# Second attention of a one-core adaLN, attention and mixture kernel: the loop over bodies of 256 tokens written anew

## What is computed

```python
def _tc_rmsnorm(x, t, gw, gb, bw, bb):
    g = (t @ gw.T + gb)[:, None, :]
    b = (t @ bw.T + bb)[:, None, :]
    inv_rms = jax.lax.rsqrt(jnp.mean(x * x, axis=-1, keepdims=True) + EPS)
    return g * x * inv_rms + b
# attention of 16 heads of 16 features, over the 64 tokens of a sequence
attn = jnp.einsum('blhd,bmhd->bhlm', q, k) / scale
p = jax.nn.softmax(attn, axis=-1)
o = jnp.einsum('bhlm,bmhd->blhd', p, v).reshape(B, L, D)
return o @ Wo.T
```

## Time and profile before

| what | us |
|---|---|
| median of 3 runs | 1128.04 |
| the three runs | 1119.44, 1128.04, 1129.88 |
| the profiled execution | 1130.07 |
| its span | 1128.4 |
| first attention, stretch of the span | 360 to 523 |
| second attention, stretch of the span | 523 to 694 |

### The profile page before, as it was taken

The page is one execution under the profiler, slowest core; times in us unless marked ns, Lnnn a source line. Parts: engine busy times, 40 slices in busy tenths (PEclk is TensorE's granted clock), DMA queues, the critical chain, the costliest instruction groups (busy, mean ns, idle before and its releaser), DMA issues. The chain is left out here.

```text
span 1128.4 us, 20924 instructions
## 1 busy us (share of the span) xinstructions
PE 929.7 (82%) x7712; PEld 792.6 (70%) x7712; DVE 651.0 (58%) x1034; ACT 525.1 (47%) x1017; POOL 194.8 (17%) x203
## 2 busy tenths in 40 slices
PE   5269999999992787884899894999988975877897
PEld 4259999999991565663677773999987862332476
DVE  2747777677760555562787875544434765221497
ACT  3046676767750233453767675333324432322332
POOL 1032232322203334421232311000000000000011
PEclk8579999999996778897999998999998976887899
DMA  8178898989951243230000000000009512999121
GB/s 317 38 250 299 317 339 301 343 324 312 336 173 42 52 141 71 49 60 21 1 1 0 0 1 1 1 1 0 1 5 354 240 65 78 410 426 381 33 72 47
DMA packets 73529, 166.57 MB, mean 148 GB/s; under 512 B 42872, under 2 KB 48248, under 8 KB 63208
## 3 DMA queue, kind: packets, MB, share of 16 engines
q1 hardware_dynamic: 62832, 122.80, 30.9%
q0 software_dynamic: 9008, 40.58, 9.8%
q10 hardware_dynamic: 1608, 2.12, 0.5%
HBM read 151.05 MB, written 12.32 MB: 145 GB/s over the span
## 5 line engine op out<-in xcount | busy, mean ns | idle before, releaser
L581 DVE TENSOR_TENSOR moew_wl<-moew_raw,moew_wh 128x1024 fp32r<-128x1024 f32 x92 | 110.1, 1220 | 21.4 <-issue 19.9
L84 PE MATMUL moe_pH<-moe_hh,moew_wh 128*128 128x256 f32 x368 | 103.2, 281 | 1.2 <-DVE moe_hl L590 1.2
L86 PE MATMUL moe_pH<-moe_hl,moew_wh 128*128 128x256 f32 x368 | 102.6, 279 | 0.0
L85 PE MATMUL moe_pH<-moe_hh,moew_wl 128*128 128x256 f32 x368 | 102.6, 279 | 0.0
L543 ACT ACTIVATE moe_ht<-moe_pH,moe_b 128x256 f32<-128x256 f32 x184 | 76.6, 467 | 39.4 <-PE moe_pH L86 39.4
L590 DVE TENSOR_TENSOR moe_hl<-moe_ht,moe_hh 128x512 fp32r<-128x512 f32 x92 | 63.8, 694 | 52.2 <-ACT moe_hh L552 51.9
L2456 POOL TENSOR_TENSOR tok_xb<-k_x,k_rows 128x512 f32<-128x512 f32 x8 | 10.2, 1272 | 425.6 <-POOLq L71 363.7
L84 PEld LDWEIGHTS moe_pH<-moe_hh,moew_wh 128*128 128x128 f32 x368 | 69.1, 188 | 1.4 <-DVE moe_hl L590 1.4
L86 PEld LDWEIGHTS moe_pH<-moe_hl,moew_wh 128*128 128x128 f32 x368 | 69.2, 188 | 0.0
L85 PEld LDWEIGHTS moe_pH<-moe_hh,moew_wl 128*128 128x128 f32 x368 | 69.0, 187 | 0.0
L528 ACT ACTIVATE moew_wh<-moew_raw 128x1024 fp32r<-128x1024 f32 x44 | 46.3, 1055 | 45.8 <-DMA moew_raw<-in_w 45.1
(11 more groups left out here) (364 smaller groups left out, 2875.3 us busy)
## 6 DMA issues: line engine op xcount, KB each, us to landing
moew_raw<-in_w SPq DMA_DIRECT2D x46, 512.0 KB
moew_wh<-in_w POOLq DMA_DIRECT2D x23, 1024.0 KB, 8.3
moew_raw<-in_w SPq DMA_DIRECT2D x23, 1024.0 KB
ring<-in_w_slot SPq DMA_DIRECT2D x11, 2048.0 KB, 19.2
...
```

The source lines that it names most:

```text
L84: nc.tensor.matmul(out, ah, bh, start=start, stop=False)
L85: nc.tensor.matmul(out, al, bh, start=False, stop=False)
L86: return nc.tensor.matmul(out, ah, bl, start=False, stop=stop)
L581: v.tensor_tensor(wl[a][l][:, n], raw_w[a][l][:, n], f32(wh[a][l][:, n]), ALU.subtract).then_inc(wl_ok[l], 1)
```

## The change

`attention_second` replaces the second attention. It takes over the three helpers of the first attention and its form of softmax.

- Scores: head masks are now 4 copies of the keys (three on VectorE, one on ScalarE), and a product covers 64 features, 64 queries and 4 heads; four such products sit in the four quarters of the array.
- Values, weights times values, and output are direct fp32 products; queries and keys stay split. The tokens are split once, not twice over, and used for queries and keys.
- Values carry a column of ones, so the same product gives the sum of the weights. VectorE takes its reciprocal and multiplies the result, which has tokens on partitions; TensorE turns the result back, ScalarE copies it, and the product with the output weights follows one body behind. GpSimd no longer divides.
- Largest, difference and exponential take all 16 heads of a tile in one step of 1024 elements.
- The output weights are loaded anew by 8 DMAs in an order that fits the new layout. The split and the copy of the old ones go.
- All 8 bodies are written out.

```diff
@@ -1060,545 +1060,375 @@
+def attention_second(nc, g, dr):
...
+        kx = sb("kx", [P, KD, HR, PB])
+        m4 = sb("m4", [P, HR])
...
+        @block.sync
+        def _(sp):
+            for r in range(4):
+                for k in range(KD):
+                    sp.dma_start(wo[32 * r:32 * r + 32, k, :], dr.wo4[64 * (r % 2):64 * (r % 2) + 32, 2 * k + r // 2, :]).then_inc(wo_in, 16)
+            sp.wait_ge(wo_in, 16 * 4 * KD)
...
+            def biased(i):
+                pool.wait_ge(u1_ok, i + 1)
+                if i > 0:
+                    pool.wait_ge(v_ps, i)
+                    pool.wait_ge(ul_ok, i)
+                nc.gpsimd.tensor_tensor(batches(u2[:, :, :]), batches(u1[:, :, :]), bc(g.ada[:, 1, :, 4 * i:4 * i + 4], 3, S), ALU.add).then_inc(u2_ok, 1)
...
-            def softmax_end(t):
-                for c in range(2):
-                    pool.wait_ge(rc_ok, 2 * t + c + 1)
-                    after(pool, pt_ps, 2 * t + c - 1)
-                    nc.gpsimd.tensor_tensor(pn[c][:, :, :], ex[c][:, :, :], bc(rc[c][:, :], 2, S), ALU.mult).then_inc(pn_ok, 1)
...
-                pe.wait_ge(k_sb, NK * (i + 1))
-                pe.wait_ge(oh_ok, 2 * t + 2)
-                pe.wait_ge(ol_ok, 2 * t + 2)
-                for j in range(4):
-                    last = mm3(nc, b2[:, 0:D], oh[:, j, :, :].rearrange("p b s -> p (b s)"), ol[:, j, :, :].rearrange("p b s -> p (b s)"),
...
+            def keys(i):
+                pe.wait_ge(uh_ok, i + 1)
+                pe.wait_ge(ul_ok, i + 1)
+                features(pC, 1).then_inc(k_ps, 1)
+
+            def queries(i):
+                if i > 0:
+                    pe.wait_ge(v_dve, i)
+                    pe.wait_ge(v_act, i)
+                features(pD, 0).then_inc(q_ps, 1)
+
+            def values(i):
+                pe.wait_ge(u2_ok, i + 1)
+                pe.wait_ge(q_sb, i + 1)
+                values_of(nc, pV, u2, g.w_small[:, W_V2]).then_inc(v_ps, 1)
+
+            def scores(t):
+                i = t // 2
+                pe.wait_ge(q_sb, i + 1)
+                pe.wait_ge(kx_dve, NM * (i + 1))
+                pe.wait_ge(kx_act, (HR - NM) * (i + 1))
+                if t >= 2:
+                    pe.wait_ge(df_ok, t - 1)
+                scores_of(nc, pS[t % 2], qT, kx, t % 2 * P, t % 2 * P).then_inc(s_ps, 1)
+
+            def turn_weights(t):
+                i = t // 2
+                pe.wait_ge(ex_ok, t + 1)
+                for n, bank in enumerate((pA, pB)):
+                    if n == 0 and t > 0:
+                        pe.wait_ge(ot_ok, t)
+                    if n == 1 and t % 2 == 0 and i >= 2:
+                        pe.wait_ge(o_sb, i - 1)
+                    if n == 1 and t % 2 == 1 and i >= 1:
+                        pe.wait_ge(oT_sb, i)
+                    for j in range(4):
+                        last = nc.tensor.transpose(four(bank)[:, j, :], ex[t % 2][:, 8 * n + 2 * j:8 * n + 2 * j + 2, :].rearrange("p h k -> p (h k)"), g.ident[:, :])
+                    last.then_inc(pt_ps, 1)
+
+            def results(t):
+                i = t // 2
+                pe.wait_ge(pt_sb, 2 * t + 2)
+                pe.wait_ge(v_dve, i + 1)
+                pe.wait_ge(v_act, i + 1)
+                results_of(nc, pR, pt, vst[i % 2], t % 2 * 2).then_inc(r_ps, 1)
+
+            def turn_results(i):
+                pe.wait_ge(ot_ok, 2 * i + 2)
+                for a in range(2):
+                    for k in range(KD):
+                        last = nc.tensor.transpose(two(pB)[:, k, a * P:(a + 1) * P],
+                                                   otm[(2 * i + a) % 4][:, 8 * k:8 * k + 8, :].rearrange("p h d -> p (h d)"), g.ident[:, :])
+                last.then_inc(ot_ps, 1)
+
+            def product(i):
+                pe.wait_ge(oT_sb, i + 1)
+                if i == 0:
+                    pe.wait_ge(wo_in, 16 * 4 * KD)
+                for a in range(2):
+                    for k in range(KD):
+                        last = nc.tensor.matmul(two(pB)[:, a, :], oT[:, k, a * P:(a + 1) * P], wo[:, k, :], start=k == 0, stop=k == KD - 1)
+                last.then_inc(o_ps, 1)
+
...
+            for i in range(NBODY):
+                t = 2 * i
+                scores(t + 1)
+                if i + 1 < NBODY:
+                    keys(i + 1)
+                turn_weights(t)
+                if i + 1 < NBODY:
+                    queries(i + 1)
+                results(t)
+                if i > 0:
+                    turn_results(i - 1)
+                if i + 1 < NBODY:
+                    scores(t + 2)
+                if i + 2 < NBODY:
+                    turn(i + 2)
+                turn_weights(t + 1)
+                if i + 1 < NBODY:
+                    values(i + 1)
+                results(t + 1)
+                if i > 0:
+                    product(i - 1)
+            pe.wait_ge(o_sb, NBODY - 1)
+            turn_results(NBODY - 1)
+            product(NBODY - 1)
...
+            def high(i):
+                act.wait_ge(u2_ok, i + 1)
+                if i > 0:
+                    act.wait_ge(q_ps, i)
+                nc.scalar.activation(uh[:, :, :], u2[:, :, :], ACT.Copy).then_inc(uh_ok, 1)
+
+            def keys(i):
+                act.wait_ge(k_ps, i + 1)
+                if i > 0:
+                    act.wait_ge(kx_dve, NM * i)
+                nc.scalar.activation(kT[:, :, :], two(pC), ACT.Copy).then_inc(k_sb, 1)
+                act.wait_ge(k_sb, i + 1)
+                act.wait_ge(m4_ok, 1)
+                if i > 0:
+                    act.wait_ge(s_ps, 2 * i)
+                for s in range(NM, HR):
+                    nc.scalar.activation(kx[:, :, s, :], kT[:, :, :], ACT.Copy, scale=m4[:, s:s + 1]).then_inc(kx_act, 1)
+
+            def queries(i):
+                act.wait_ge(q_ps, i + 1)
+                if i > 0:
+                    act.wait_ge(s_ps, 2 * i)
+                nc.scalar.activation(qT[:, :, :], two(pD), ACT.Copy).then_inc(q_sb, 1)
...
+            def weights(t):
+                for n, bank in enumerate((pA, pB)):
+                    act.wait_ge(pt_ps, 2 * t + n + 1)
+                    if t > 0:
+                        act.wait_ge(r_ps, t)
+                    nc.scalar.activation(pt[:, 4 * n:4 * n + 4, :], four(bank), ACT.Copy).then_inc(pt_sb, 1)
+
+            def exps(t):
+                act.wait_ge(df_ok, t + 1)
+                if t >= 2:
+                    act.wait_ge(pt_ps, 2 * (t - 1))
+                nc.scalar.activation(ex[t % 2][:, :, :], df[t % 2][:, :, :], ACT.Exp, scale=SCALE).then_inc(ex_ok, 1)
+
+            def results_turned(i):
+                act.wait_ge(ot_ps, i + 1)
+                if i > 0:
+                    act.wait_ge(o_ps, i)
+                nc.scalar.activation(oT[:, :, :], two(pB), ACT.Copy).then_inc(oT_sb, 1)
...
+            for i in range(NBODY):
+                t = 2 * i
+                if i + 1 < NBODY:
+                    keys(i + 1)
+                weights(t)
+                if i + 1 < NBODY:
+                    queries(i + 1)
+                exps(t + 1)
+                if i + 2 < NBODY:
+                    scaled(i + 2)
+                if i > 0:
+                    results_turned(i - 1)
+                weights(t + 1)
+                if i + 2 < NBODY:
+                    high(i + 2)
+                if i + 1 < NBODY:
+                    exps(t + 2)
+                    values(i + 1)
+                if i > 1:
+                    squares(i - 2)
+            squares(NBODY - 2)
+            results_turned(NBODY - 1)
+            squares(NBODY - 1)
...
-                    n = 2 * t + c
-                    dve.wait_ge(ex_ok, n + 1)
-                    after(dve, rc_ok, n - 1)
-                    v.tensor_reduce(sm[c][:, :], ex[c][:, :, :], AX_X, ALU.add).then_inc(sm_ok, 1)
...
+            def adapt(i):
+                dve.wait_ge(x_ps, i + 1)
+                if i > 0:
+                    dve.wait_ge(u2_ok, i)
+                v.tensor_tensor(batches(u1[:, :, :]), batches(two(pC)), bc(g.ada[:, 0, :, 4 * i:4 * i + 4], 3, S), ALU.mult).then_inc(u1_ok, 1)
+
+            def low(i):
+                dve.wait_ge(uh_ok, i + 1)
+                v.tensor_tensor(ul[:, :, :], u2[:, :, :], f32(uh[:, :, :]), ALU.subtract).then_inc(ul_ok, 1)
+
+            def masked(i):
+                dve.wait_ge(k_sb, i + 1)
+                if i > 0:
+                    dve.wait_ge(s_ps, 2 * i)
+                for s in range(NM):
+                    v.tensor_scalar(kx[:, :, s, :], kT[:, :, :], m4[:, s:s + 1], None, ALU.mult).then_inc(kx_dve, 1)
...
+            def softmax(t):
+                a = t % 2
+                dve.wait_ge(s_ps, t + 1)
+                v.tensor_reduce(mx[a][:, :], pS[a][:, :, :], AX_X, ALU.max).then_inc(mx_ok, 1)
+                dve.wait_ge(mx_ok, t + 1)
+                if t >= 2:
+                    dve.wait_ge(ex_ok, t - 1)
```

(35 more changed lines are left out.)

529 lines of the change are left out of this document (102 added, 427 removed).

## The result

The changed kernel takes 1083.52 us in the median of 4 runs (1080.17 to 1087.79), the kernel before 1128.96 beside it (4 runs): a ratio of 0.9617, 95% interval 0.9554 to 0.968. The forecast was 1090, its range 1083 to 1112. The profiled execution took 1084.33 us at a span of 1082.5, 45.9 less than the 1128.4 of the earlier trace rows.

The account below looks back on a forecast made before the run. TensorE was taken to bound the second attention, VectorE close behind. Opening 13.9, TensorE work 106, waits 3.3, 1.8 and 4.5, last steps 2.0 gave 131.5 us, 37.8 less than 169.3: kernel 1090 us, range 1083 to 1112.

Parts of the forecast that it names:

- first case: Forecast as summed: second attention falls from 169.3 to 131.5 us, kernel to 1090 us; chance 0.58.
- A body: 256 tokens of the second attention: TensorE's work sums to 14.0 us, against 17.46 before.
- Opening: Start of the second attention up to its first scores: 13.9 us.
- The second keys: Body 0 of the second attention waits some 2.5 us for the second token group's low part on VectorE.
- End: Second attention's last tiles, turn and product wait about 4.5 us for other engines; last addition and squares take 2.0.
- The turn of the tokens in steady bodies: Second attention: TensorE waits for tokens scaled late on ScalarE, 0.3 us per body for 6 bodies, 1.8 us.
- The stage: The whole second attention takes 131.5 us, 37.8 less than 169.3.
- The other stages: Stages before and after the second attention keep work, code and transfers: zero change in length.
- the chain: Rival, 0.17: VectorE, GpSimd and ScalarE steps before the next keys bound second-attention bodies, 15 to 16 us; kernel 1097 to 1104.
- The clock: Rival, 0.12: TensorE's clock falls in each second-attention body; at 0.87 its 106 us grow by 16, kernel 1106.
- The late arrivals: Rival, 0.09: first attention's late pickup of scores comes with its helpers; second-attention body 18.8 us, kernel 1122.
- The low level: Rival, 0.04: TensorE's clock stays low for most of the second attention; at 0.60, 71 us more, kernel 1161.

## Why the prediction was right

Its first case came true, at the very edge of its range: 1083.52 us against a lower bound of 1083. By its own steps:

- **A body**: 14.0 summed, 14.00 measured. The terms too: scores 2.05 (2.12 taken), keys and queries 3.32 (3.24), values 1.80, weights times values 2.06 (2.02), turn of the weights 1.76 (1.84), turns of the results and of the tokens 1.08 (1.16), output 1.93 (1.83). The bound was read rightly: what is added to TensorE's work appears in the time, what is added to VectorE's does not. The Trainium skill (TensorEngine Tiling (Array Packing), Theoretical Speedup) has a factor of up to 2 for a contraction of 64 or less on top of column tiling; here it was 1.8, from 1.94 to 1.09 us by the rows, and from 1.87 to 1.03 by the start of what follows.
- **Opening**: 13.9 forecast, 13.8 measured (520.5 to 534.27). **The second keys**: 2.5 forecast, 2.43 measured. The 0.8 that stood beside them was for the next turn, which waited 0.15; a wait of 0.79 did come, but for the low part before the third keys (551.20), which the prediction did not have. That the two agree is luck. **End**: waits of 4.5 forecast, 3.4 measured (0.74, 0.33, 0.74, 0.79, 0.77), then 1.7 instead of 2.0.
- **The turn of the tokens in steady bodies**: 1.8 us forecast, none measured. This step failed: ScalarE scales the tokens behind the exponential at 598.63 to 599.5, and TensorE reaches the turn at 599.93. It does not wait.
- **The stage**: 131.5 forecast, 128.8 measured: 1.8 less for the turn, 1.4 less at the end, and 0.6 more of TensorE's own work (106.6 for 106).
- **The other stages**: zero forecast, 5.3 us measured. Their code is the same. The trace of before is one of the four with late signals in the first attention (122.0 us from first to last scores), that of after is clean (117.4); so 3.5 us are within what that stage does by itself. The 1.8 us behind the stage are within what the same code varies by there, 428.7 to 437.5 us over the traces. Profiled execution: 1092.3 forecast, 1084.33 measured; 2.7 + 3.5 + 1.8 = 8.0. Two thirds of the miss thus do not come from the change, and a few tenths more would have put the time outside the range.

The rivals: **the chain** had a margin of 1 us by forecast, 1.2 by measurement, and did not decide. What was thinner than forecast is the copy of the turned weights: half a microsecond was taken, and for the first tile it is 0.05 (597.21 to 597.26). The run with four masked copies on ScalarE ran into just this. **The clock** did not fall in the change, but the run with the output in its own body shows that rival at work in this very stage: waits of 2.35 and 0.69 us, and 0.50 behind them. I had put it at a mean loss from the first attention. These runs give no length of wait from which it decides: in the changed kernel the clock is 1.00 from 540 to 550 us, behind the 2.43 us at 538.66; behind the same wait it is 0.50 at 543 to 545 us in the run with the values twice; and with the scores in two tiles only some of the waits of 1.94 us brought it down. So whether the change kept its clock there was a matter of 1.4 us either way. **The late arrivals** did not come with the helpers; they belong to the gathers, as was blamed. But the gathers cost in two ways: by a queue on GpSimd, in every trace that has the masked copy ahead of them, and by signals of TensorE that VectorE and ScalarE take up late, in some traces only. The changed kernel's own trace has none of the late signals, in the first attention neither, so it alone does not refute this rival. The late traces do: with the output split and with the two tiles and the weights first, signals are up to 4.5 us late in the first attention and at most 0.07 us in the second, with the same helpers. The price put on this rival is a slip besides: 18.8 less 14.0 is 4.8 a body, not 4.5, so 1124 and not 1122. **The low level** did not occur: 1.00 in the steady body.

What the change owes to which part is shown only in part. The scores with their fewer copies are worth 29.7 us of the stage, while the rest stands as it is; the sums left out and the wide steps nothing that shows in a body; the unsplit output product costs 0.3 us a body. Moving the output into its own body costs 36.1 us, but that is no step back to the kernel before, so it is the price of a worse order and not a part of the 40.5. The new form of the values (1.80 us for 3.2 a body by the rows), the halved number of output products and the waits of 1.65 us that fell away were not undone by any run.
